# A mixer, attention and feed-forward block on one core: the last score products interleaved, Silu in one pass, GpSimd's scale and offset moved

## The reference

```python
# token mixer: x -> q, k, v; windowed weights ew = exp(w_bias * mask)
num = einsum('ts,nsd->ntd', ew, exp(k) * v);  den = einsum('ts,nsd->ntd', ew, exp(k))
h = (sigmoid(q) * num / den) @ out_w + out_b + flatten(x)
h = layernorm(h) * ln_g + ln_b
h = concatenate([cls_tok, h])                        # 257 tokens

# attention, 16 heads of 64, on layernorm(h)
attn = softmax(q @ k.T * 64 ** -0.5)
attn = einsum('bhij,hg->bgij', attn, reattn_w)       # heads mixed
attn = (attn - mean_over_heads) * rsqrt(var_over_heads + 1e-3) * gamma + beta
h = h + (attn @ v) @ w_out + b_out

# feed-forward, inputs quantised to 8 bits per row, weights to -1, 0, 1
gate = silu(bitlinear(layernorm(h), w_gate))         # 256 -> 1024
h = h + bitlinear(gate * bitlinear(layernorm(h), w_up), w_down)
```

## Time and profile before

| | |
|---|---|
| median of 3 runs | 884.55 us (881.21 to 884.91) |
| profiled execution | 881.73 us |
| its span, first to last instruction | 879.9 us |
| granted TensorE clock, mean | 0.924 |
| TensorE busy (matmuls) | 702.9 us, 80% |
| VectorE busy | 599.9 us, 68% |
| ScalarE busy | 436.0 us, 50% |
| GpSimd busy | 212.0 us, 24% |
| chain that ended last | TensorE 46%, VectorE 25%, ScalarE 12%, issue 7%, DMA 7%, GpSimd 3% |

### The profile page before, as it was taken

How to read it: one execution, slowest core, us unless ns; L and a number is a source line. 1 busy time by engine, 2 the same in 40 slices (tenths; PEclk the granted TensorE clock), 3 DMA queues, 4 the chain that set the end, 5 groups by cost and what they waited for, 6 DMA issues and landing times.

```text
span 879.9 us, 18945 instructions
## 1 busy us (share of the span) xinstructions
PE 702.9 (80%) x7634; PEld 479.6 (55%) x7634; DVE 599.9 (68%) x1266; ACT 436.0 (50%) x1230; POOL 212.0 (24%) x399
## 2 busy tenths in 40 slices
PE   0759648988798888987898979888898789768654
PEld 0436435756475746664575647564676457535421
DVE  0596559568955886678856895578767885659444
ACT  0104617472648256654647264825665464828310
POOL 0308134012510233015301251024301540033000
PEclk9969889999999989998998999998999889989877
DMA  8301460145104610262114510461026200450000
GB/s 313 148 1 30 163 216 3 35 159 198 32 1 158 227 38 1 90 222 82 31 48 150 195 32 1 152 233 39 2 85 206 101 8 27 167 198 9 1 12 0
DMA packets 42395, 83.98 MB, mean 95 GB/s; under 512 B 3003, under 2 KB 6596, under 8 KB 41668
## 3 DMA queue, kind: packets, MB, share of 16 engines
q1 hardware_dynamic: 41268, 79.29, 26.4%
q10 hardware_dynamic: 1040, 3.49, 1.0%
HBM read 46.98 MB, written 35.79 MB: 94 GB/s over the span
## 4 chain that ended last, share of the span: by engine, by line
PE 46%; DVE 25%; ACT 12%; issue 7%; DMA 7%; POOL 3%; SPq 0%; POOLq 0%; ACTq 0%; DVEq 0%
PE big L560 6%; PE big L543 6%; PE small L543 6%; PE small L699 6%; DMA pg<-turned 4%; DVE an L1275 3%; ACT pst L930 3%; DVE var L1231 3%; PE small L684 3%; DMA turned<-pst 3%; ACT ot L1018 3%; PE big L729 2%; PE big L483 2%; PE big L632 2%; PE small L654 2%
## 5 line engine op out<-in xcount | busy, mean ns | idle before, releaser
L930 ACT ACTIVATE pst<-big,nb 128x256 f32<-128x256 f32 x256 | 117.6, 473 | 32.1 <-DVE nb L1201 32.1
L1198 DVE TENSOR_REDUCE mx<-big 128x4 f32<-128x1024 f32 x64 | 78.3, 1223 | 49.6 <-PE big L560 49.0
L632 PEld LDWEIGHTS big<-pst,pg 64*64 64x64 f32 x4096 | 70.1, 142 | 58.3 <-DVE an L1275 35.3
L632 PE MATMUL big<-pst,pg 64*64 64x64 f32 x4096 | 78.7, 230 | 26.5 <-DVE an L1275 19.3
L560 PE MATMUL big<-qk_t 64*128 64x256 f32 x512 | 72.6, 402 | 11.2 <-ACT qk_t L913 11.2
L1275 DVE TENSOR_TENSOR an<-big,rstd 128x1024 f32<-128x1024 f32 x64 | 78.4, 1224 | 2.2
L1231 DVE TENSOR_REDUCE var<-sqb 128x64 f32<-128x1024 f32 x64 | 76.9, 1210 | 4.2 <-ACT sqb L950 4.0
L950 ACT ACTIVATE sqb<-big 128x1024 f32<-128x1024 f32 x64 | 65.2, 1020 | 28.3 <-PE big L632 26.2
L654 PE MATMUL small<-w_qkv,xnv 128*128 128x512 f32 x128 | 70.2, 675 | 8.0 <-DVE h L1375 4.2
L543 PE MATMUL small<-xnt,w_qkv 128*128 128x256 f32 x256 | 63.8, 392 | 0.0
L560 PEld LDWEIGHTS big<-qk_t 64*128 64x128 f32 x512 | 44.1, 186 | 36.1 <-issue 17.7
(11 more groups left out here) (201 smaller groups left out, 1306.9 us busy)
## 6 DMA issues: line engine op xcount, KB each, us to landing
turned<-pst SPq DMA_DIRECT2D x128, 257.0 KB
pg<-turned SPq DMA_DIRECT2D x16, 2056.0 KB, 10.9
w_qkv<-in_w_qkv SPq DMA_DIRECT2D x1, 3072.0 KB
xt<-in_x_t SPq DMA_DIRECT2D x8, 256.0 KB, 3.1
xr<-in_x_tok SPq DMA_DIRECT2D x8, 256.0 KB, 2.8
out<-h SPq DMA_DIRECT2D x16, 128.0 KB
an<-in_gate_t ACTq DMA_DIRECT2D x1, 1024.0 KB, 8.9
an<-in_up_t ACTq DMA_DIRECT2D x1, 1024.0 KB, 11.2
```

The costliest lines, as they stand in the source:

```text
L632: last = mm(mix_place(n)[half[0]:half[1], k_hi * 512 + i * 64:k_hi * 512 + (i + 1) * 64], pg[rows, ib, j], w_rows[rows, it, ib, :], start= ...
L930: last = A(pst[:, g % 2, h % GH, it * T:(it + 1) * T], big[p % 2][:, (j * TT + it) * T:(j * TT + it + 1) * T], ACT.Exp, bias=nb[:, h, it:i ...
L1198: V.reduce_max(mx[:, hs, :], big[p % 2][:, :].rearrange("p (h t l) -> p h t l", h=2, t=TT), AX)\
```

## The change

**GpSimd.** `mixer_affine` is merged into `mixer_out`: scale and offset now stand right behind rs_a, at the end of the iteration, ahead of the Newton step of group 0.

The core of the diff:

```diff
+        def turned_x(ahead):
+            return bank2_bf[:, T * 2:T * 2 + MC * P] if ahead else big0_bf[:, 0:MC * P]
...
@@ TensorE: scores @@
                     if p < HP - 1:
                         qk(p + 1)
+                    elif before_last:
+                        before_last()
                     dots(p)
@@ TensorE: mix_heads @@
-                    pe.wait_ge(ff["dve"].sem, ff["dve"].at(b - 1, (("t", "hh")[n - 1], 1)))
+                    if n == 1:
+                        pe.wait_ge(ff["act"].sem, ff["act"].at(b - 1, ("silu", 1)))
+                    else:
+                        pe.wait_ge(ff["dve"].sem, ff["dve"].at(b - 1, ("hh", 1)))
@@ TensorE: turn_x, gate_up @@
-                    elif not is_(b, B - 1):
-                        pe.wait_ge(act_s.sem, act_s.at(b + 1, ("e", HP - 2)))
...
-                    for k, w in enumerate((w_gate, w_up)):
-                        if k and st is ff and tt == 0 and not is_(b, B - 1):
-                            pe.wait_ge(act_s.sem, act_s.at(b + 1, ("e", HP - 1)))
+                    for k in parts:
+                        w = (w_gate, w_up)[k]
+                        if st is ff and tt == 0 and not is_(b, B - 1):
+                            pe.wait_ge(act_s.sem, act_s.at(b + 1, ("e", HP - 2 + k)))
@@ TensorE: iteration @@
-                    scores(b + 1, lambda: project(b, 0))
+                    scores(b + 1, lambda: project(b, 0), (lambda: mixer_kv(b + 2, [0])) if do_mixer else None)
...
                 turn_x(0)
-                gate_up(0)
+                if do_mixer:
+                    mixer_kv(b + 2, [1])
+                attend(b, 1, 0)
+                gate_up(0, [0])
+                attend(b, 1, 1)
+                gate_up(0, [1])
                 if do_scores:
                     turn_class(b + 1)
-                if do_mixer:
-                    mixer_kv(b + 2)
-                for g in range(NO):
-                    attend(b, 1, g)
+                attend(b, 1, 2)
+                attend(b, 1, 3)
@@ ScalarE @@
-            def ffn_tanh(b, st, rows, tt):
+            def ffn_silu(b, st, rows, tt):
+                if tt == 0:
+                    nc.scalar.preload_act_table_set("silu_and_others")
                 act.wait_ge(st["pe"].sem, st["pe"].at(b, ("g", tt)))
-                act.wait_ge(st["dve"].sem, st["dve"].at(b, ("cgh", tt)))
-                A(sqb[0:rows, tt, :], big[0][0:rows, :], ACT.Tanh, scale=cg_half[0:rows, tt:tt + 1])\
+                act.wait_ge(st["dve"].sem, st["dve"].at(b, ("cg", tt)))
+                A(sqb[0:rows, tt, :], big[0][0:rows, :], ACT.Silu, scale=cg[0:rows, tt:tt + 1])\
                     .then_inc(st["act"].sem, 1)
@@ VectorE: scores, ffn_quant, ffn_h @@
+                    if p == HP - 1 and after_last:
+                        after_last()
                     if p:
                         total(p - 1)
...
-                V.tensor_scalar(cg_half[r, c], cg[r, c], 0.5, None, ALU.mult).then_inc(s.sem, 1)
...
-                V.tensor_tensor(cgu[r, c], cg_half[r, c], cu[r, c], ALU.mult).then_inc(s.sem, 1)
...
-                dve.wait_ge(st["act"].sem, st["act"].at(b, ("tanh", tt)))
-                V.scalar_tensor_tensor(out=w, in0=w, scalar=1.0, in1=big[0][r, :], op0=ALU.add, op1=ALU.mult)\
-                    .then_inc(s.sem, 1)
-                dve.wait_ge(s.sem, s.at(b, ("t", tt)))
+                dve.wait_ge(st["act"].sem, st["act"].at(b, ("silu", tt)))
                 dve.wait_ge(st["pe"].sem, st["pe"].at(b, ("gu", tt)))
                 V.tensor_tensor(w, big[1][r, :], w, ALU.mult).then_inc(s.sem, 1)
@@ GpSimd @@
             def mixer_out(b):
                 power(b, pool_a, dve_a, ve_a, rs_a, P, slice(0, TT), "ve")
-
-            def mixer_affine(b):
                 pool.wait_ge(dve_a.sem, dve_a.at(b, ("n", 1)))
...
-                    if n == 0 and do_scores:
-                        mixer_affine(b + 1)
-                    elif n == 3 and do_scores:
+                    if n == 3 and do_scores:
                         mixer_norm(b + 1)
```

More of the change, by code:

```diff
@@ L224, in build @@
         cg = sb("cg", [P, TT])
-        cg_half = sb("cg_half", [P, TT])
-        cgu = sb("cgu", [P, TT])
         ah = sb("ah", [P, TT])
@@ L270, in ffn_stages @@
             each = range(tiles)
-            x_part = ["st", "ag", "ve", "n", "am", "amc", "sx", "q1", "q2", "cg", "cgh", "cu", "cgu"]
-            h_part = ["t", "hh", "ah", "th", "s2", "s2u", "cd", "r1", "r2"]
+            x_part = ["st", "ag", "ve", "n", "am", "amc", "sx", "q1", "q2", "cg", "cu"]
+            h_part = ["hh", "ah", "th", "s2", "s2u", "cd", "r1", "r2"]
             return dict(
                 pe=stage(f"pe_{tag}", [(x, tt) for tt in each for x in ("xt", "g", "gu", "ht", "dn")]),
-                act=stage(f"act_{tag}", [(x, tt) for tt in each for x in ("xt", "tanh", "ht")]),
+                act=stage(f"act_{tag}", [(x, tt) for tt in each for x in ("xt", "silu", "ht")]),
                 dve=stage(f"dve_{tag}", [(x, 0) for x in x_part + h_part] + [(x, tt) for tt in each[1:] for x in x_part]
@@ L453, in _, with mixer_kv @@
             mm = nc.tensor.matmul
-            def mixer_kv(b):
+            def mixer_kv(b, tiles=range(TT)):
                 pe.wait_ge(s_xt, 16 * (b + 1))
-                for st in range(TT):
+                for st in tiles:
                     for c in range(MC):
@@ L508, in mixer_turn, with scores @@
                 last.then_inc(pe_a.sem, 1)
-            def scores(b, first_project=None):
+            def scores(b, first_project=None, before_last=None):
                 pe.wait_ge(act_a.sem, act_a.at(b, "xt"))
@@ L704, in turn_x @@
                 def turn_x(tt):
+                    ahead = st is ff and tt == 0 and not is_(b, B - 1)
                     if tt:
@@ L857, in _ @@
             setup_totals()
-            scores(0)
+            scores(0, None, lambda: mixer_kv(1, [0]))
+            mixer_kv(1, [1])
             turn_class(0)
-            mixer_kv(1)
             mixer_q(1)
@@ L1052, in iteration @@
                     ffn_x(b, ff, P, 0)
-                ffn_tanh(b, ff, P, 0)
-                attend(b, 1, 0)
                 if do_mixer:
                     mixer_exp(b + 2)
-                for g in range(1, NO):
+                ffn_silu(b, ff, P, 0)
+                for g in range(NO):
                     attend(b, 1, g)
@@ L1163, in mixer_norm, with scores @@
                 norm_apply(b, dve_a, h2, xn, P, range(TT), mv_a, rs_a, pool_a, "rs2")
-            def scores(b, first=None, between={}):
+            def scores(b, first=None, between={}, after_last=None):
                 dve.wait_ge(pe_s.sem, pe_s.at(b, "class"))
@@ L1357, in ffn_h @@
                 dve.wait_ge(s.sem, s.at(b, ("ah", tt)))
-                V.tensor_scalar(hm[r, c], ah[r, c], cgu[r, c], QEPS, ALU.mult, ALU.max).then_inc(s.sem, 1)
+                V.tensor_scalar(hm[r, c], ah[r, c], cu[r, c], QEPS, ALU.mult, ALU.max).then_inc(s.sem, 1)
                 dve.wait_ge(s.sem, s.at(b, ("th", tt)))
@@ L1384, in first @@
                         ffn_stats(b, ff, P, 0, h3_0)
-                    scores(b + 1, first, {0: lambda: ffn_norm(b, ff, P, 0), 1: lambda: ffn_quant(b, ff, P, 0)})
+                    scores(b + 1, first, {0: lambda: ffn_norm(b, ff, P, 0), 1: lambda: ffn_quant(b, ff, P, 0)},
+                           (lambda: mixer_in(b + 2)) if do_mixer else None)
                 else:
@@ L1505, in _ @@
             then(V.reciprocal(w_scale, w_mean[:]))
-            scores(0)
-            mixer_in(1)
+            scores(0, None, {}, lambda: mixer_in(1))
             mixer_y(1)
```

24 lines of the change are left out of this document (10 added, 14 removed).

## The result

The changed kernel takes 851.48 us in the median of four runs (847.55 to 854.99); the kernel before took 884.61 beside it. The ratio is 0.9633, 95% interval 0.9576 to 0.9689.

What follows compares the result with a forecast made beforehand. Busy times named no single bound; the chain of waits showed three places: scores' end, second feed-forward tile, start of mixing. 7.3 + 12.5 + 2.2 + 1.3 = 23.3 us off 881.73 gave 858.4; plus 1.1, 859.5, range 853 to 870.

Steps and rivals of the forecast that it cites:

- Term A: Start of mixing: group 0's rstd, slowed beside GpSimd's scale, drops from 1.27 to 0.23 us, seven times: 7.3 us.
- in ScalarE's order: Mixer's tanh on ScalarE: runs from Silu's table set with no further load, so loads stay at two per iteration.
- The new wait of TensorE: End of the scores: TensorE waits 1.8 us before attend 2 for ScalarE's ot; sums still start 1.6 us earlier.
- rival (b): Sums after the new TensorE wait: clock falls to 1.2 GHz, 10 us lost in six iterations, 868.6 us; chance 0.10.
- Rival (c): VectorE's reductions beside GpSimd's scale and offset are held by the shared port: 883 us, no change; chance 0.05.
- rival (a): Second tile: VectorE's bias additions delay pair 6's writes, so the gather lands 1.7 us later: 866.8 us; chance 0.11.
- would mostly not recur: End of the scores: half clock on up and its neighbours mostly vanishes once waits are filled; 2.5 us taken against 2.3.
- The 853 at the low end: Low end of the forecast range, in us: the case that half-clock stretches vanish as well.
- Five iterations at 2.5: Second feed-forward tile, iterations 0 to 4, with slack in the gather: 2.5 us each, 12.5 in all.
- L1350 wait for up: Second tile, iteration 2: VectorE's product starts once up ends, at 403.85 instead of 406.16, 2.3 us won.
- Iterations 5 and 6 were priced at 1.1 each: Second tile: the gather is already on the chain, so only removing VectorE's L1346 counts, 2.2 us in all.
- The 1.1 us put on top: Whole kernel: added to 858.4 us because the profiled execution, 881.73, was low against the median of 884.55.

Runs made afterwards that it cites:

- warm: The changed kernel plus 14 and 8 small unused TensorE products per iteration, filling its waits at the start of mixing: 850.1 us, ratio 0.9622.
- only_pool: The kernel before with only GpSimd's scale and offset moved ahead of its Newton steps: 868.3 us, ratio 0.9788.
- undo_pe: The changed kernel with the old order at the end of the scores on TensorE, ScalarE and VectorE: 873.1 us, ratio 0.9872.
- only_silu: The kernel before with only Silu in place of tanh and VectorE's extra step, orders untouched: 882.7 us, ratio 0.9964.
- late_in: The changed kernel with VectorE's mixer_in behind the last row total instead of ahead of it: 854.3 us, one run.
- before_warm: The kernel before plus 14 and 8 small unused TensorE products per iteration at the start of mixing: 873.5 us, ratio 0.9875.
- late_scales: The changed kernel with the second tile's row scales behind the mixer's output and GpSimd's second half of the weights behind rs_a: 851.6 us, ratio 0.9638.

## Why the prediction was wrong

**What held.** The direction, and the mechanism of every part. Term A: all seven rstd of 1.27 us became 0.23; the six in H to N brought 5.8 us, the missing 0.5 being the last iteration's half clock (6.3 in warm and only_pool). The handover to GpSimd held nothing up. Silu's pass is tanh's. Table loads per iteration stayed at two, and the sentence that they do "in ScalarE's order" carried more than I saw: without that order they are four in six iterations (undo_pe, only_silu). The new wait of TensorE was 1.94 us (1.8 forecast), and the sums took 3.62 to 3.69 us in all six iterations (3.69 in the same view before), so rival (b) as priced is out. But what it feared came in one iteration of six: in iteration 0 the clock fell behind that wait, for 3.4 us over the next attend products (in warm, in three of six):

```profile
195.03 1.56 PE L692 MATMUL small<-an,v 128*64 128x128 f32 x16 [1.93 <-ACT ot L1029]
196.28 2.02 PE L692 MATMUL big<-an,v 128*64 128x128 f32 x16
```

The sums followed M by 34.0 us there instead of 32.6, and the landing of the gather, later still, hid it. Rival (c) is out by the reductions at 1.21, rival (a) by the landings and late_in. The gather is waited for in thirteen places, far more than the "more than five" of the forecast.

**The step that failed** is the one on the clock: that half-clock stretches "would mostly not recur" was given 0.2 us per iteration, and only at the end of the scores. The clock weighed more, and elsewhere. Before lost some 11 us to half clock that small products could win back, most of it between N and the next M (202.0 against 193.5 in the traces), where my sum has no term at all. The change shortens TensorE's wait ahead of group 0's successor from 2.12 to 1.08 us, by the very stall that term A counts, and keeps 31.7 us of that stage in four iterations of six. With the small products in both kernels the gain is 23.3 us, without them 33. That 23.3 is also the forecast's sum is chance: between the traces of before_warm and warm it is made up otherwise (M to H 13.0, H to N 6.3, N to M 1.8, start 2.4, end 0.3). The 853 at the low end stood for the clock too, and was 1.5 us short. The term could have been read in the trace of before: N to M lasts 32.7 to 34.4 us there, and a stretch at 1.2 GHz stands in it in every iteration.

**Sizes within M to H.** Five iterations at 2.5 gave 12.5; measured 14.5 (264.9 to 250.4). In iteration 2 the size was near (2.3 forecast, 2.6 measured) and the bound another. The forecast had L1350 wait for up, at M + 49.9, with up's products at the 1.91 us of the earlier trace rows. That was half clock: they took 1.03 after, up ended at M + 48.0, and the gather, landing at M + 47.4, was last with its 2.3 us of VectorE work. Iterations 1, 3 and 4 won 3.2, 3.3 and 3.4, where before the end of the scores ran at half clock (the second tile's `h<-small,hold` at 43.7, 44.2 and 43.8 us behind M, 42.3 in its best). Iterations 5 and 6 were priced at 1.1 each as gather-bound: measured 3.2 and -0.1. H follows the landing in both, but the landing itself moved, 48.9 to 47.0 in iteration 5 and 47.1 to 47.8 in iteration 6. A landing that differs by a microsecond between executions was taken for a property of the iteration; the two together, 3.1, are near the 2.2.

**The level.** The 1.1 us put on top for the run level went the wrong way: the profiled execution of before was a low one, that of after the highest of four. The stretches at the start of mixing are the likely reason, since the runs of warm hardly differ; only one execution of each kernel was traced.

**What stays open.** Setup lost 2.4 us, with a stretch at 1.2 GHz from 113.7 to 130.8 us in after; no run was made for it, and the same stage reads 162.5 to 166.7 over all the kernels. Why the clock falls in iterations 0 and 3 and holds in 2 after the same waits isn't shown either. How much the clock costs in all isn't known: no run holds it everywhere. And the parts don't add up (16.5, 18.8 and 3.2 alone, 32.5 together; undone one by one 11.4, 10.5 and 21.1): the loads of Silu explain a part of it, the clock is the likely rest, which is argued from the traces and not separated.

## What to carry to other kernels

Look at every stage with TensorE's granted clock beside it, also those that a change doesn't touch: a wait made a microsecond shorter can hold the clock for the work behind it. Here about 10 of the 33 us went when small products filled such waits in both kernels. When parts of a change share an engine's order, price them as one, and look for what each needs ahead of it (table set, operands); undoing one may create a cost that neither kernel had. Once an engine's wait is filled, name the transfer behind it and its engines' busy share: at 92% of 16 engines it is the next bound.

## What the runs showed of the hardware

- Silu over 128x1024 takes 1.11 us, as tanh. It shares no table set with Exp: each change between them is a load of 1.28 us. The load starts 0.03 us behind the activation before it (374.15 + 0.70), and the activation behind it 0.01 us after its end (376.17 after 374.88 + 1.28), so that is the whole price. The Trainium skill, page "ScalarE: Activation LUTs", section "What ACT_TABLE_LOAD costs", gives the same 1283 ns but adds 1380 ns of drain to every switch; these traces show no such time, and the measurement decides.
- A VectorE instruction of 128x2 elements took 0.50 us (L1123 at 397.84) beside GpSimd's weights at 396.27 to 398.31, and 0.17 in late_scales where GpSimd was idle; L1336 took 1.17 beside them there and 0.35 in after. So one-input tensor_scalar instructions were held beside GpSimd too, and seven rstd of 1.04 us are left in the kernel after (at 427.0, for one, beside GpSimd's copy of xnv); the reductions of 1.21 us never were.
- The gather of 2 MB runs at 332 GB/s with the DMA engines 92% busy, and its landing behind M has nearly the same mean in before, after and late_in (47.6 to 47.8 us), with a scatter of about 1 us from one iteration to the next.
- Same waits (0.83 and 1.08 us), same products, other clock: 2.4 GHz in iteration 2 and 1.2 GHz in iteration 0 of one execution. With 0.94 us of small products between them, which left 0.31 and 0.29 us of wait, it stayed at 2.4 GHz in iteration 0 of warm.
